# Layer 0's weight splits on ScalarE: context keys centred and split elsewhere, pieces and stores placed elsewhere

## The reference

```
ln_out = _ln(hidden_states, ln_w, ln_b)
q  = _ln(fp8_linear(ln_out, wq),  qln_w, qln_b)      # 8 groups x 2 heads x 128
k  = _ln(fp8_linear(ln_out, wk),  kln_w, kln_b)      # 8 groups x 128
v  = fp8_linear(ln_out, wv)
core = softmax(q k^T / sqrt(128)) v
qx = _ln(fp8_linear(ln_out, wqx), qxln_w, qxln_b)
kx, vx = split(cond @ w_kv_x^T)                      # the context's keys and values
xout = softmax(qx _ln(kx)^T / sqrt(128)) vx
out = fp8_round(concat(core, xout) / smooth) @ wproj^T * scales
```

## Time and profile before

| what | value |
|---|---|
| median of 3 timed executions | 1945.66 us (1945.54 to 1946.34) |
| the profiled execution | 1939.38 us, span 1937.2 us |
| busy share of the span | PE 89%, DVE 78%, ACT 72%, POOL 71% |
| layer 0's attention | about 90 to 1250 us of the span |
| TensorE's mean granted clock | 0.963 of full speed |

### The profile page before, as it was taken

How to read it: one execution, slowest core, us unless ns; L and a number is a source line. 1 busy time by engine, 2 the same in 40 slices (tenths; PEclk the granted TensorE clock), 3 DMA queues, 4 the chain that set the end, 5 groups by cost and what they waited for, 6 DMA issues and landing times. The chain is left out here.

```text
span 1937.2 us, 45587 instructions
## 1 busy us (share of the span) xinstructions
...
## 2 busy tenths in 40 slices
...
GB/s 155 86 166 174 172 189 184 180 200 178 175 169 196 177 187 200 209 196 185 195 222 204 192 207 165 176 146 44 1 69 2 36 2 2 2 2 2 1 2 22
DMA packets 539531, 245.74 MB, mean 127 GB/s; under 512 B 505392, under 2 KB 512560, under 8 KB 537648
## 3 DMA queue, kind: packets, MB, share of 16 engines
...
...
## 5 line engine op out<-in xcount | busy, mean ns | idle before, releaser
L2436 ACT ACTIVATE P<-score 128x1024 f32<-128x1024 f32 x384 | 365.6, 1025 | 86.3 <-PE score L2522 86.1
L1722 PE MATMUL score<-KK,QT 128*128 128x512 bf16 (+2 forms) x1920 | 346.7, 325 | 24.0 <-DVE mxp L1213 22.5
L1742 PE MATMUL pv<-PT,VV 128*128 128x256 bf16 (+1 forms) x2880 | 338.3, 274 | 4.8 <-DMA PT<-PB 4.5
L2234 POOL TENSOR_TENSOR l_rr<-l_rr,mhalf 128x32 f32<-128x32 f32 (+1 forms) x60 | 329.0, 5484 | 5.0
L1742 PEld LDWEIGHTS pv<-PT,VV 128*128 128x128 bf16 (+1 forms) x2880 | 279.6, 98 | 71.7 <-issue 31.3
L1476 ACT ACTIVATE PB<-S,rsum 128x1024 bf16<-128x1024 f32 (+1 forms) x256 | 246.3, 988 | 100.6 <-DVE rsum L1245 95.5
L1236 DVE SCALAR_TENSOR_TENSOR PB<-S,rsum,PB 128x1024 bf16<-128x1024 f32 (+1 forms) x256 | 314.3, 1228 | 2.6 <-ACT PB L1476 2.5
L1722 PEld LDWEIGHTS score<-KK,QT 128*128 128x128 bf16 x1920 | 161.2, 99 | 165.0 <-DVE mxp L1213 30.6
L1466 ACT ACTIVATE S<-S,nmx 128x1601 f32<-128x1601 f32 x128 | 209.8, 1639 | 29.9 <-DVE nmx L1227 29.9
L2540 PE MATMUL pv<-P,V 128*9 128x256 f32 (+1 forms) x3328 | 224.7, 385 | 0.0
L1038 POOL TENSOR_SCALAR S<-S,rsum 128x256 f32<-128x256 f32 x128 | 122.6, 958 | 81.3 <-DVE rsum L1245 81.3
...
## 6 DMA issues: line engine op xcount, KB each, us to landing
...
```

The lines of the kernel that those rows point to most:

```text
L1722: i = e.matmul(m.score[:, at:at + b - a], qt[:, kind, qp, q * P:(q + 1) * P], kk[:, kp, a:b], start=(k == 0), stop=(k == 2))
L1742: i = e.matmul(m.pv[:, at:at + 256], vv[0:rows, v, t, :], m.PT[k % 2][0:rows, turned(c, a), :], start=(c == first and r == 0), stop=(c == ...
L2234: e.tensor_tensor(rr, rr, m.mhalf[0:rows, 0:NH1], ALU.pow).then_inc(s["l1_rr"], 1)
L2436: e.activation(pr[:, :], bank, ACT.Exp, scale=float(D1) ** -0.5).then_inc(s["l1_exp"], 1)
```

## The change

In groups 2 to 7 the centring and the split of the context's keys leave VectorE and GpSimd. ScalarE sums each row of both kinds of keys with an accumulating ACTIVATE (`act_mean_weights`, scale -1/128; the written values go to the tile of low parts, where the real ones come later), adds the mean as a bias (`act_centre_weights`), and copies the context keys' high part; VectorE makes their low part. So there are five parts in these groups, V, KX, K, QX, Q, where KX has no scale, and the semaphores count 10 for a group and not 8 (`parts_before`), GpSimd's 2 and not 4 (`plain_before`). GpSimd keeps the context's values, now ahead of `key_norm` in the middle of the even iteration.

ScalarE's copies of the contexts' pieces stand behind `exponentials(4*it+1)` or `query_high(it+1, 1)` and no longer ahead of them. The stores of contexts 0, 1 and 3 begin at iterations 6, 10 and 26 and no longer at 3, 7 and 24. The feed-forward weights come in four halves, two in iteration 24 and two in 25.

```diff
@@ -60,6 +60,8 @@
 KINDS = (("q", "wq", CQ, 256), ("qx", "wqx", CQX, 256), ("k", "wk", CK, 128), ("v", "wv", CV, 128))
 
 QX, K, Q, V = (CQX, 256, 1), (CK, 128, 2), (CQ, 256, 0), (CV, 128, 3)
+
+KX = (CKX, 128, None)
 
 SEMS = """
 pe_end act_end dve_end pool_end sp_end
@@ -332,7 +334,7 @@
 
 def parts_of(g):
 
-    return (QX, K, Q, V) if g < 2 else (V, K, QX, Q)
+    return (QX, K, Q, V) if g < 2 else (V, KX, K, QX, Q)
 
 
 def wait_weights(e, s, g, c0):
@@ -345,10 +347,20 @@
 
 def wait_split(e, s, g, keys):
 
-    e.wait_ge(s["w_hi"], 8 * g + (4 if keys else 8))
-    e.wait_ge(s["w_hi_pool"], 4 * (g + 1))
-    e.wait_ge(s["w_lo_dve"], 8 * g + (4 if keys else 8))
-    e.wait_ge(s["w_lo_pool"], 4 * (g + 1))
+    e.wait_ge(s["w_hi"], parts_before(g + 1) if not keys else parts_before(g) + 6)
+    e.wait_ge(s["w_hi_pool"], plain_before(g + 1))
+    e.wait_ge(s["w_lo_dve"], parts_before(g + 1) if not keys else parts_before(g) + 6)
+    e.wait_ge(s["w_lo_pool"], plain_before(g + 1))
+
+
+def parts_before(g):
+
+    return 8 * min(g, 2) + 10 * max(g - 2, 0)
+
+
+def plain_before(g):
+
+    return 4 * min(g, 2) + 2 * max(g - 2, 0)
 
 
 def wait_stored(e, s, g, keys):
@@ -522,10 +534,10 @@
     wait_weights(e, s, g, c0)
     if part == 0:
         e.wait_ge(s["w_cent"], g + 1)
-        if g >= 2:
-            wait_stored(e, s, g, True)
+    if g >= 2:
+        wait_stored(e, s, g, True)
     for ic in range(IC):
-        n = 4 * g + IC * part + ic
+        n = plain_before(g) + IC * (part if g < 2 else 0) + ic
         e.tensor_copy(out[:, 0, ic, :], raw[:, ic, :]).then_inc(s["w_hi_pool"], 1)
         e.wait_ge(s["w_hi_pool"], n + 1)
         e.tensor_tensor(out[:, 1, ic, :], raw[:, ic, :], out[:, 0, ic, :], ALU.subtract).then_inc(s["w_lo_pool"], 1)
@@ -610,7 +622,10 @@
     c0, width, n = parts_of(g)[k]
     out, raw = split_weights(m, g, c0, width), raw_weights(m, g, c0, width)
     for ic in range(IC):
-        e.wait_ge(s["w_hi"], 8 * g + IC * k + ic + 1)
+        e.wait_ge(s["w_hi"], parts_before(g) + IC * k + ic + 1)
+        if n is None:
+            e.tensor_tensor(out[:, 1, ic, :], raw[:, ic, :], out[:, 0, ic, :], ALU.subtract).then_inc(s["w_lo_dve"], 1)
+            continue
         e.scalar_tensor_tensor(out[:, 1, ic, :], raw[:, ic, :], m.win[:, n * IC + ic:n * IC + ic + 1], out[:, 0, ic, :],
                                ALU.mult, ALU.subtract).then_inc(s["w_lo_dve"], 1)
 
@@ -702,13 +717,38 @@
     c0, width, n = parts_of(g)[k]
     out, raw = split_weights(m, g, c0, width), raw_weights(m, g, c0, width)
     wait_weights(e, s, g, c0)
-    if g >= 2 and k % 2 == 0:
-        wait_stored(e, s, g, c0 == CV)
-    if c0 == CK:
+    if g >= 2 and k == 3:
+        wait_stored(e, s, g, False)
+    if c0 in (CK, CKX):
         e.wait_ge(s["w_cent"], g + 1)
     for ic in range(IC):
+        if n is None:
+            e.copy(out[:, 0, ic, :], raw[:, ic, :]).then_inc(s["w_hi"], 1)
+            continue
         e.activation(out[:, 0, ic, :], raw[:, ic, :], ACT.Copy, scale=m.win[:, n * IC + ic:n * IC + ic + 1]).then_inc(
             s["w_hi"], 1)
+
+
+def act_mean_weights(e, m, s, g):
+
+    keys, out = raw_weights(m, g, CK, 2 * D), split_weights(m, g, CK, 2 * D)
+    wait_weights(e, s, g, CK)
+    wait_stored(e, s, g, True)
+    for ic, k in itertools.product(range(IC), range(2)):
+        at = slice(k * D, (k + 1) * D)
+        i = e.activation(out[:, 1, ic, at], keys[:, ic, at], ACT.Copy, scale=-1.0 / D,
+                         accum_out=m.wsum[g % 2][:, ic, k:k + 1])
+    i.then_inc(s["w_sum"], 1)
+
+
+def act_centre_weights(e, m, s, g):
+
+    keys = raw_weights(m, g, CK, 2 * D)
+    e.wait_ge(s["w_sum"], g + 1)
+    for ic, k in itertools.product(range(IC), range(2)):
+        at = slice(k * D, (k + 1) * D)
+        i = e.activation(keys[:, ic, at], keys[:, ic, at], ACT.Identity, bias=m.wsum[g % 2][:, ic, k:k + 1])
+    i.then_inc(s["w_cent"], 1)
 
 
 def act_context_high(e, m, s, b, ic):
@@ -787,7 +827,7 @@
 SPLIT_AT = {14: ((2, 0), (2, 1), (2, 2)), 19: ((3, 0),), 20: ((3, 1),), 21: ((3, 2),)}
 INPUTS_AT = {14: 2, 22: 3}
 
-STORES_AT = (3, 7, 15, 24)
+STORES_AT = (6, 10, 15, 26)
 
 EARLY = (B - 1) * TB
 
...
+        if 3 * G <= it < 3 * G + 2:
+            sp_raw_up(e, m, s, it - 3 * G, 0)
...
@@ -1086,6 +1128,8 @@
             pool_split_weights(e, m, s, 1, 0)
             pool_round_end(e, m, s, 4)
             pool_split_weights(e, m, s, 1, 1)
+        if 0 <= it < SPLITS and it % 2 == 0:
+            pool_split_weights(e, m, s, it // 2 + 2, 1)
         for b, i in SPLIT_AT.get(it, ())[0:1]:
             pool_piece_low(e, m, s, b, i)
         key_norm(it + 1)
@@ -1102,11 +1146,7 @@
             pool_layernorm(e, m, s, 2, EPS5, 0, EARLY)
         split_self(4 * it + 2)
         take_magnitudes(2 * it - 2)
-        if 0 <= it < SPLITS and it % 2 == 0:
-            pool_split_weights(e, m, s, it // 2 + 2, 0)
         magnitudes(2 * it - 1)
-        if 0 <= it < SPLITS and it % 2 == 0:
-            pool_split_weights(e, m, s, it // 2 + 2, 1)
         add_magnitudes(2 * it - 1)
 
 
@@ -1323,8 +1363,6 @@
         scaled(4 * it + 2, 0)
         smooth(2 * it - 1)
         p_lo(4 * it + 1, 0)
-        if 0 <= it < SPLITS and it % 2 == 0:
-            dve_sum_weights(e, m, s, it // 2 + 2)
         squares_out(it + 1)
         if it == -1:
             dve_round_start(e, m, s, 5)
@@ -1334,14 +1372,12 @@
             dve_weights_low(e, m, s, 1, 2)
         scaled(4 * it + 2, 1)
         scaled(4 * it + 2, 2)
-        if 0 <= it < SPLITS and it % 2 == 0:
-            dve_centre_weights(e, m, s, it // 2 + 2)
         values_low(it + 1, 1)
         if it == -1:
             dve_weights_low(e, m, s, 1, 3)
         offset(4 * it + 2)
         if 0 <= it < SPLITS:
-            dve_weights_low(e, m, s, it // 2 + 2, 2 * (it % 2))
+            dve_weights_low(e, m, s, it // 2 + 2, 3 * (it % 2))
         if it == NGB - 1:
             dve_normalise(e, m, s, 2, m.x, m.f_xn, 0, EARLY)
         query_full(it + 1, 1)
@@ -1364,8 +1400,11 @@
         if it == -1:
             dve_round(e, m, s, 7)
         offset(4 * it + 3)
-        if 0 <= it < SPLITS:
-            dve_weights_low(e, m, s, it // 2 + 2, 2 * (it % 2) + 1)
+        if 0 <= it < SPLITS and it % 2 == 0:
+            dve_weights_low(e, m, s, it // 2 + 2, 1)
+            dve_weights_low(e, m, s, it // 2 + 2, 2)
+        elif 0 <= it < SPLITS:
+            dve_weights_low(e, m, s, it // 2 + 2, 4)
         p_lo(4 * it + 2, 0)
         if it == NGB - 1:
             dve_turned_low(e, m, s, 1)
@@ -1510,9 +1549,9 @@
         keys_high(it + 1, 3)
         if it == -1:
             act_weights_high(e, m, s, 1, 1)
+        exponentials(4 * it + 1)
         for b, i in SPLIT_AT.get(it, ())[0:1]:
             act_piece_high(e, m, s, b, i)
-        exponentials(4 * it + 1)
         p_hi(4 * it + 1, 0)
         query_norm(it + 1, 1)
         if it == -1:
@@ -1523,6 +1562,8 @@
         if it == -1:
             act_scaled_inputs(e, m, s, 6)
         p_hi(4 * it + 1, 1)
+        if 0 <= it < SPLITS and it % 2 == 0:
+            act_mean_weights(e, m, s, it // 2 + 2)
         if it == NGB - 1:
             act_raw_high(e, m, s, 1)
         if it == NGB:
@@ -1532,16 +1573,21 @@
             act_up(e, m, s, 0)
             act_up(e, m, s, 1)
         values_high(it + 1, 1)
+        query_high(it + 1, 1)
         for b, i in SPLIT_AT.get(it, ())[1:]:
             act_piece_high(e, m, s, b, i)
-        query_high(it + 1, 1)
         if 0 <= it < SPLITS:
-            act_weights_high(e, m, s, it // 2 + 2, 2 * (it % 2))
+            act_weights_high(e, m, s, it // 2 + 2, 3 * (it % 2))
+        if 0 <= it < SPLITS and it % 2 == 0:
+            act_centre_weights(e, m, s, it // 2 + 2)
         values_high(it + 1, 2)
         norms_out(it + 1)
         exponentials(4 * it + 2)
-        if 0 <= it < SPLITS:
-            act_weights_high(e, m, s, it // 2 + 2, 2 * (it % 2) + 1)
+        if 0 <= it < SPLITS and it % 2 == 0:
+            act_weights_high(e, m, s, it // 2 + 2, 1)
+            act_weights_high(e, m, s, it // 2 + 2, 2)
+        elif 0 <= it < SPLITS:
+            act_weights_high(e, m, s, it // 2 + 2, 4)
         if it == NGB - 1:
             act_turned(e, m, s, 0)
         values_high(it + 1, 3)
@@ -1823,12 +1869,12 @@
     e.dma_start(m.brow[:, :], m.A["ffn_bias"].partition_broadcast(P)).then_inc(s["ffn_in"], 16)
 
 
-def sp_raw_up(e, m, s):
+def sp_raw_up(e, m, s, k, part):
 
     e.wait_ge(s["pa_full"], made(3 * G - 1, "V3"))
     e.wait_ge(s["ctx_out"], 192)
-    for k in range(2):
-        e.dma_start(m.raw[k][:, :], raw_parts(m)[k][0]).then_inc(s[f"wp_in{k}"], 16)
+    at = slice(part * WIDE // 2, (part + 1) * WIDE // 2)
+    e.dma_start(m.raw[k][:, at], raw_parts(m)[k][0][:, at]).then_inc(s[f"wp_in{k}"], 16)
 
 
 def sp_reload(e, m, s):
```

6 lines of the change are left out of this document (3 added, 3 removed).

## The result

The kernel after takes 1919.89 us (median of 4 runs, 1919.57 to 1924.55) against 1945.6 us before on the same chip (4 runs, 1943.47 to 1946.34): a ratio of 0.9884, 95% interval 0.9867 to 0.9901. That is 25.7 us faster; 1920.0 was predicted. Its profiled execution took 1919.57 us (span 1917.4).

What follows compares the result with a forecast made beforehand. GpSimd's late split was taken to stall TensorE in iterations 2 to 11. Savings of 23.0 + 2.1 + 0.8 - 0.2 = 25.7 us took 1945.7 to 1920; range 1907 to 1933, most likely 1913 to 1926 (0.64).

Steps and rivals of the forecast that it cites:

- The bound and the stall: Iterations 2 to 11: GpSimd, 4.3 us late from its split, makes TensorE wait 3.51 us for kn; about 8.5 per pair.
- GpSimd's place: Even iteration: the values' split, 2.5 us, fits GpSimd's 2.53 us wait ahead of rr; 0.1 charged for rr.
- Rival (e): Values' split ahead of rr waits for the load of rawh or the store before it: slower, 1950 to 1960; chance 0.05.
- Four small ones: VectorE, from the context-key subtractions to the next scores: 5.0 + 1.1 less some 0.3 makes 5.8 us, as now.
- double blocking: Even iteration: VectorE's new pair could meet GpSimd's catq and ym one after the other, some 1.2 us longer.
- ScalarE: Added work per split: sums 1.6 us, hidden in a wait for TensorE; centring 1.3, copies 0.6, partly hidden by waits.
- V3: Last values' piece, from ScalarE about 1.7 us later; VectorE waits some 0.4, of which 0.3 is charged to the even iteration.
- The odd iteration: Slow clock (1.5 us) goes, the wait for mxp grows to 2.4: 34.8 + 2.4 = 37.2 us, 1.3 less than now.
- rival (c): Odd iteration's mxp wait stays at 1.8 without the slow clock: pair 71.3, time 1907 to 1913; chance 0.11.
- 3.57 - 1.8 + 0.6: Odd iteration's mxp wait: iteration 1's 3.57, less 1.8 of TensorE's projection products, plus 0.6 for VectorE's addition: 2.4 us.
- A pair: Even plus odd iteration of the split phase: 36.3 + 37.2 = 73.5 us against 78.1; five pairs give 23.0.
- Pieces, loads, stores: Context pieces behind exp or query copy save 2.1 us (0 to 4), halved feed-forward loads save 0.8, moved stores cost 0.2.

Runs made afterwards that it cites:

- 8 columns: Kernel after, with VectorE's two subtractions of the context keys cut to 8 columns of 128 from the second group on: 1919.1 us, ratio 0.9876.

## Why the prediction was right, step by step

**The bound and the stall.** Right, and shown: GpSimd's late split bounded the even iteration; moving it without touching VectorE's work wins, and lightening VectorE without moving it wins 2.5 in the phase, most of it in iteration 5, where half clock stayed away (4.3 by the medians, a little more than I expected).

**GpSimd's place.** Right: rr starts no later (charged 0.1, measured none), and the statistics start at 32.15 us behind TQ0, predicted 31.3, since VectorE's a_mv came later than I thought. Rival (e) had no occasion.

**VectorE: the term that was mis-sized.** "Four small ones, 0.34 each less an overlap", less a wait beside catq that was to be theirs instead of p_lo's, should have kept this place at 5.8 us; it takes 6.75, and the even iteration came out at 36.84 for 36.3. Counted from start to start, against the iteration without splits (4.96), two things make up the difference. The four small ones take 2.37, since the second waits for catq, and the first p_lo is 1.11 shorter for it, as I had said: together 1.26 more, where 0.8 was charged. The other half, 0.5, is the second p_lo, 1.39 us long for 0.87: without the split ahead of it GpSimd's yt comes earlier, and this p_lo now meets it (the same with 8 columns, 1.38 us long). For that the prediction had no term; no run moved yt alone. I had double blocking as a bound ("some 1.2 us longer"), but with catq and ym, and gave it too little weight.

**ScalarE.** Sums: four in 1.3 us where 1.6 was charged; centring 1.27 for 1.3; copies 0.48 for 0.6. All hidden: VectorE does not wait for V3, for which 0.3 had been charged.

**The odd iteration.** 36.99 for 37.2, and a wait for mxp of 1.84 for 2.4. It stayed as before (1.82), as rival (c) had it; which term of 3.57 - 1.8 + 0.6 is off no run shows. But the clock did not stay at 1.00 in every execution: iteration 9's wait of 2.20 was followed by half clock in most, where I had said that 2.4 to 2.8 did not lower it elsewhere. In before the one wait of that size, 2.77 at 668.34, did not; of the nine profiles that have this wait for kn half clock followed in four. A pair: 73.8 (74.2 for 8 and 9, 75.9 with the slow clock) for 73.5. Five pairs gave 19.8 to 21.1 in the phase for 23.0.

**Pieces, loads, stores.** Predicted 2.1, 0.8 and -0.2. Measured by lengths: the pieces nothing that can be told in iterations 13 to 15, where 0.9 and more was expected, and 1.2 in 19 to 21, the halves about 2, the stores nothing that can be told. By the medians all three together gave 0.9902 - 0.9884 = 0.0018, 3.5 us, across two chips.

**The sum.** 25.7 was predicted and 25.7 measured, but to this agreement luck has its part. The prediction took the profiled execution down to 1913.7 and added 6.3, the distance of the median of before from its own; the profiled executions of after took 1919.57 and 1921.88, 5.9 and 8.2 above, and the medians of their runs were 1919.9 and 1917.5. So the saving in the profiled execution was overestimated, and a distance that did not recur made it good. The spans are 1937.2 and 1940.4 before, 1917.4 and 1919.8 after, 20.2 less on average. Of this the phase gives 20.4, the pieces 1.1, the halves 2.9 and iteration 30, which was not foreseen, 3.3. Lost are 1.3 ahead of iteration 2, 1.4 in 13 to 15, and 3.8 behind iteration 31's first exp (703.5 and 703.7 against 707.4 twice; the nine profiles with the whole split have 704.0 to 707.9). And 1.0 is lost in iteration 12, which takes 36.4 to 36.6 in all nine with the whole split and 35.4 or 35.5 in the others: TensorE waits 1.28 us there for a DMA transpose in the first profile after, 0.13 in before's, a price of the split that the prediction did not have.

Both profiles of before lie below its medians of 1943.9 to 1945.7, by 1 and 6 us, within its spread of 1938.4 to 1951.5. Which stretch makes the usual run of before longer than its profiled ones stays open; by the table a later row in iterations 13 to 15 is one candidate, which was not tested.
